# One pipeline over six layers: attention tiles and feed-forward groups interleaved, queries normalised on GpSimd, row maxima subtracted by a product on TensorE

## The reference, cut to what matters

```python
x = x + linear_attention(layernorm(x))            # once, 4 x 1024 tokens of 128
y = layernorm(x)
for i in range(6):
    y = attn_layer(shift_tokens(y), ...) + y
    y = ffn_layer(shift_tokens(y), ...) + y
return x + y

def attn_layer(x, Wqkv, qs, ksc, Wo):             # 16 heads of 64
    q, k, v = split(x @ Wqkv)
    q = l2norm(q) * qs;  k = l2norm(k) * ksc
    q = q*cos*scale + rotate_half(q)*sin*scale    # k with 1/scale
    sim = einsum(q, k) * 8                        # windows of 32, with the window before
    attn = softmax(where(mask, -max, sim))
    return einsum(attn, v).reshape(...) @ Wo

def ffn_layer(x, g, bln, W1, b1, W2, b2):         # inner width 341
    xn = layernorm(x) * g + bln
    a, gate = split(xn @ W1 + b1)
    return a * gelu(gate) @ W2 + b2
```

## Time and profile before

| | |
|---|---|
| median of 3 runs | 3576.26 us (3575.43 to 3576.86) |
| the profiled execution | 3575.57 us, span from first to last instruction 3573.7 us |
| PE busy | 3252.6 us, 91% |
| ACT busy | 2933.6 us, 82% |
| DVE busy | 2791.6 us, 78% |
| POOL busy | 2045.7 us, 57% |
| granted TensorE clock, mean | 0.958 of full speed |

### The profile page before, as it was taken

How to read it: one execution, slowest core, us unless ns; L and a number is a source line. 1 busy time by engine, 2 the same in 40 slices (tenths; PEclk the granted TensorE clock), 3 DMA queues, 4 the chain that set the end, 5 groups by cost and what they waited for, 6 DMA issues and landing times. The chain is left out here.

```text
span 3573.7 us, 118257 instructions
## 1 busy us (share of the span) xinstructions
PE 3252.6 (91%) x42076; PEld 2208.0 (62%) x42076; DVE 2791.6 (78%) x5370; ACT 2933.6 (82%) x9257; POOL 2045.7 (57%) x2150
## 2 busy tenths in 40 slices
PE   5699998889999789999789999978999977999977
PEld 4466665656666556666566666665666655666656
DVE  7788887578888568888658888757888856888865
ACT  3399998479999459999649999937999955999973
POOL 3566665456666356666446666545666634666644
PEclk8799999899999899999899999989999989999999
DMA  2000001100000100000110000010000010000011
GB/s 70 10 7 8 7 7 33 22 13 7 7 7 6 47 15 8 7 7 7 37 24 7 8 7 7 10 44 14 7 8 7 6 43 19 8 7 7 7 34 42
DMA packets 141061, 57.58 MB, mean 16 GB/s; under 512 B 118598, under 2 KB 137668, under 8 KB 139460
## 3 DMA queue, kind: packets, MB, share of 16 engines
q1 hardware_dynamic: 140484, 50.01, 5.9%
HBM read 22.57 MB, written 2.10 MB: 7 GB/s over the span
## 5 line engine op out<-in xcount | busy, mean ns | idle before, releaser
L1321 ACT ACTIVATE probs<-s_ps,nbias,rnorm 128x64 f32<-128x64 f32 x3072 | 1229.9, 447 | 1.6 <-DVE nbias L1039 0.9
L1524 POOL TENSOR_TENSOR qk_rot<-by_cos,by_sin 128x1024 f32<-128x1024 f32 x384 | 914.0, 2380 | 381.9 <-DVE by_sin L989 334.8
L597 PE MATMUL ring<-wvo,xsT 128*32 128x512 f32 x6144 | 794.8, 600 | 10.2 <-ACT vo L1144 10.2
L1321 ACT ACTIVATION_READ_ACCUMULATOR probs<-s_ps,nbias,rnorm 128x1 f32 x3072 | 765.0, 249 | 0.0
L1513 POOL TENSOR_TENSOR probs<-probs,rrow 128x256 f32<-128x256 f32 x768 | 454.6, 613 | 429.1 <-DVE rrow L973 429.1
L986 DVE TENSOR_TENSOR by_cos<-qk_ps,rotary 128x1024 f32<-128x1024 f32 x378 | 463.0, 1225 | 147.1 <-ACT squares L1307 147.1
L1533 POOL TENSOR_TENSOR qk_rot<-qk_rot,rnorm 128x1024 f32<-128x1024 f32 x192 | 365.5, 1904 | 341.4 <-DVE rnorm L733 341.4
L543 PEld LDWEIGHTS ring<-cst,qk_rot 128*128 128x128 f32 x3072 | 341.3, 141 | 243.7 <-ACT vo L1144 155.9
L543 PE MATMUL ring<-cst,qk_rot 128*128 128x128 f32 x3072 | 446.4, 278 | 27.6 <-POOL qk_rot L1524 24.4
L1001 DVE TENSOR_REDUCE sumsq<-squares 128x16 f32<-128x1024 f32 x384 | 462.9, 1206 | 0.0
L989 DVE TENSOR_TENSOR by_sin<-qk_ps,rotary 128x1024 f32<-128x1024 f32 x378 | 459.2, 1215 | 0.0
(11 more groups left out here) (166 smaller groups left out, 5433.4 us busy)
## 6 DMA issues: line engine op xcount, KB each, us to landing
qk_rot<-L_ffn_Wqkv SPq DMA_DIRECT2D x7, 1024.0 KB, 5.1
xs<-x_tok SPq DMA_DIRECT2D x194, 32.0 KB
xs<-x_tok SPq DMA_DIRECT2D x194, 31.8 KB
by_cos<-x_tok SPq DMA_DIRECT2D x48, 128.0 KB
by_cos<-x_tok SPq DMA_DIRECT2D x48, 127.0 KB
wv<-L_ffn_Wqkv SPq DMA_DIRECT2D x7, 512.0 KB, 6.6
wo_pad<-L_ffn_Wo SPq DMA_DIRECT2D x14, 256.0 KB, 7.3
xs<-x_tok SPq DMA_DIRECT2D x194, 0.2 KB
```

The lines of the kernel that those rows point to most:

```text
L597: last = mm(r[WIN * mh:WIN * (mh + 1), :], xsT[:, a, WIN * w:WIN * (w + 1)], wvo[:, mh, :, :], start=True, stop=True)
L1321: last = nc.scalar.activation(probs[:, a, h // 4, :, h % 4, :], s_ps[:, half, c:c + 2 * WIN].rearrange("p (s c) -> p s c", s=2), ACT.Exp, ...
L1524: g.tensor_tensor(qk_rot[:, n, :], by_cos[:, n, :], by_sin[:, n, :], ALU.add).then_inc(added[qk], 1)
```

## The change

The loop over layers is gone; every engine's list is written out for all of the program, 202 steps. A step still has the parts of the attention tiles, and now also parts of feed-forward groups: group U starts in step 6 + 4U, three steps after its last tile entered (the step in which that tile's residual is added), and moves through eight steps, while attention goes on with later tiles of the same layer and of the next. A step of kind f (0 to 3) is a step `6 + 4U + f`; kind 0 and 4 of one group fall together, and so on.

```diff
+        def group(k, f):
+            u, rest = divmod(k - LAST_RESIDUAL - f, FT)      # 6 + f, 4
+            return u if rest == 0 and 0 <= u < GROUPS else None
...
+                down(group(k, 6))
+                up("gate", 2, group(k, 3))
+                project("k", 0, 1)
+                project("k", 1, 1)
+                for part, at_step in NEXT_VALUES:            # steps 14, 15, 18, 19, 22, 23 of a layer
+                    next_values(next_layer_at(k, at_step), part)
+                values(2, 2)
+                transposed("q", 1, 2)
+                transposed("q", 0, 2)
+                values(1, 2)
+                transposed("k", 0, 2)
+                up("up", 0, group(k, 3))
+                up("up", 1, group(k, 3))
+                values(0, 2)
+                transposed("k", 1, 2)
+                probs_transposed(0, 3)
+                xs_transposed(0)
+                scores(0, 2)
+                normalised_transposed(group(k, 2))
+                project("q", 0, 0)
+                project("q", 1, 0)
+                up("up", 2, group(k, 4))
+                probs_transposed(1, 3)
+                values(3, 2)
+                scores(1, 2)
+                shift(0, 2)
+                output(3)
+                up("gate", 0, group(k, 2))
+                up("gate", 1, group(k, 2))
+                shift(1, 2)
```

The softmax is put together otherwise. DVE writes the negated row maxima, PE adds them to the scores in PSUM, ACT takes the exponentials with no scale, bias or sum, four heads at a time, and DVE sums the rows. The query norms can then no longer be the exponential's scale, so POOL multiplies the queries by them:

```diff
+                def shift(half, s):
+                    pe.wait_ge(max_done[half], done(T))
+                    mm(s_ps[:, half, :], ident_r[:, :], nmax[:, 8 * half:8 * half + 8].unsqueeze(2)
+                       .broadcast_to([P, 8, 2 * WIN]), start=False, stop=True, ...).then_inc(shifted[half], 1)
...
-                        for h in (h0, h0 + 1):
+                    act.wait_ge(shifted[half], done(T))
+                    for q in range(2):
+                        last = nc.scalar.activation(
+                            probs[:, a, 2 * half + q].rearrange("p s h c -> p h s c"),
+                            s_ps[:, half, 256 * q:256 * q + 256].rearrange("p (h s c) -> p h s c", h=4, s=2), ACT.Exp)
...
+                def row_sums(half, s):
+                    dve.wait_ge(exp_done[half], done(T))
+                    v.tensor_reduce(psum_row[...], p, AXY, ALU.add).then_inc(row_summed[half], 1)
...
-                    add_rotated("q", 0)
-                    add_rotated("k", 0)
-                    normalise_k(0)
-                    normalise(0, 1)
-                    normalise(1, 1)
+                normalise(1, 2)
+                add_rotated("q", 0)
+                next_wqk_lower(next_layer_at(k, NT - 1), 0)
+                squared4(group(k, 0))
+                normalise_rotated("q", 0)
+                add_rotated("k", 0)
+                x_and_bias(group(k, 2))
+                normalise_rotated("k", 0)
+                group_rsqrt(group(k, 0))
+                normalise(0, 1)
+                next_wqk_lower(next_layer_at(k, NT - 1), 1)
```

1516 lines of the change are left out of this document (756 added, 760 removed).

## The result

| | before | after |
|---|---|---|
| median | 3576.45 us (4 runs) | 3762.48 us (4 runs, 3761.50 to 3763.90) |
| ratio | | 1.0521, 95% interval 1.0503 to 1.0539 |
| span of the profiled execution | 3573.7 us | 3761.5 us |
| PE, ACT, DVE, POOL busy | 91, 82, 78, 57% | 93, 61, 81, 65% |
| mean granted clock | 0.958 | 0.984 |

The changed kernel is 5.2% slower. The forecast of 3512 us is missed by 250 us, and the range (3370 to 3690) by 72.

The account below looks back on a forecast made before the run. PE and ACT both full in attention; the prize was 122.8 us a layer outside it. Front 148, 48 groups of 67.9 (3259), values 22, seam 30, ramps 51: 3510 us of span, 3512 us forecast; eight in ten 3370 to 3690.

Parts of the forecast that it names:

- The failed step on DVE: On DVE, the second small operation comes 0.08 us before POOL's pair ends and was expected to go in between.
- the rival with 0.27: DVE's small operations wait for the port POOL holds: a miss costs PE 1.5 us, 3600 to 3795 us; chance 0.27.
- The failed step on PE: On PE, a tile keeps its pieces at 14.00 us and gets two shifts, becoming 14.6 us.
- the two shifts: On PE, two added products of 512 columns a tile, 0.31 us each, 0.62 together.
- the waits besides the port: PE held 1.3 us for the group's token scaling and 0.6 for gelu's table load, per four tiles.
- what is paid once a layer: At each layer's seam: next layer's values 4.5 us, five times 22; POOL's weight splitting 30 us in all.
- The late scaling in the step of kind 2: POOL's sum delays DVE's scaling of the group's tokens, holding PE's transposes 1.3 us; bounds 0 and 3.4.
- Gelu's table: On ACT, the load ahead of gelu delays the keys' squares; 0.6 us charged a group, bounds 0 and 1.28.
- A group's own products: On PE, a feed-forward group's transposes, W1 and W2 products: together 7.5, say 7.6 us.
- A period above 69.2 us: Sign on PE: four tiles and a group taking longer than this make the kernel slower than before; 67 to 69 expected.
- the 95% given: Sign: PE busy above 95% through the whole middle, with ACT and POOL at 70 to 75%.
- the sign named for the rival: PE waiting at L573 for DVE's rotation would show the slower port rival, chance 0.27.

Follow-up runs that it names:

- e1: Changed kernel with DVE's first two small operations of the inverse norms moved ahead of the reciprocal that POOL waits for: 3621.2 us, 1.0130 to before.
- e14: Changed kernel with PE's order of e6, everything else as it was, DVE's small operations too: 3707.7 us, 1.0367 to before.
- e18: e12 with queries projected ahead of the group's token transposes on PE, but DVE's small operations ordered as in the changed kernel: 3640.9 us, 1.0187 to before.
- e6: e5 with values 1 moved on PE directly behind values 2, ring order and ACT's copies to match: 3550.4 us, 0.9938 to before.
- e7: e6 with gelu replaced by the square, which needs no table of its own (output differs): 3521.7 us, 0.9856 to before.
- e5: e1 with PE's first-half shift ahead of the second half's scores and the last values behind them, joining the last blocks: 3589.0 us, 1.0042 to before.
- e12: e6 with ACT's copy of the transposed tokens moved ahead of the queries' squares, and three buffers for them: 3500.0 us, 0.9790 to before.

## Why the prediction was wrong, point by point

**The failed step on DVE.** "It comes 0.08 us before POOL's pair ends, and then I expect it to go in between." The mechanism and the place were in the text as the rival with 0.27; the order of two events 0.08 us apart was guessed from pitches of other pairs of instructions. The first small operation starts 0.19 us behind the reciprocal and not 0.12, and POOL's sum 1.41 behind it and not 1.46, so L785 comes 0.02 to 0.05 us after the sum instead of 0.08 before it. In 154 of 192 steps it takes 2 us or so; in 31 of the 48 steps of kind 2 it is ahead of the sum and stays short. It costs 141 us (e1), 157 and 164 by e14 and e18: 0.73 to 0.85 us a step, half of the 1.5 that the rival had. The Trainium skill ("SBUF — State Buffer", Who interferes with whom) says that whoever issues first holds the shared pair for the whole instruction. By that rule, the trace agrees: 2.38 us when POOL's sum is first, 0.18 when POOL is idle. Where L785 starts less than 0.02 us ahead of the sum, the trace has both outcomes, 14 times each.

**The failed step on PE.** "A tile keeps its pieces and gets two shifts." The pieces were kept, not their neighbours. With 14 changes of shape instead of 6 they cost 14.73 us and not 14.0; the changes that the two shifts bring lift those from 0.62 to 0.71. Against 16.5 us a tile e1 shows 17.31: 0.81 x 192 = 155 us. It could be read before: mask to scores is 0.31 us (407.09 to 407.40 in the earlier trace rows), projection to projection 0.24:

```profile
405.29 0.40 PE L531 MATMUL qk_ps<-wqk_hi,xsT_lo 128*128 128x512 f32 x1
405.53 0.39 PE L529 MATMUL qk_ps<-wqk_hi,xsT_hi 128*128 128x512 f32 x1
```

I took the first for the price of a product standing alone, and so the shift, 0.31 forecast and 0.35 in e1, came out about right for another reason. With this step failed and the small operations first (e1) the kernel is 1.3% slower than before; with the port's waits alone on top of the forecast (3512 + 141 = 3653) it would have been slower as well, and e18, with PE's better order, is 1.9% slower.

**The sum.** 3510 of span; PE's pace +155, the port's waits +141; against it the waits besides the port: 1.9 us a group were charged, and in e1's last layer PE's gaps are 2.00 us in four groups, 0.5 each, -67. That makes 3739, and 22 us of the span of 3761.5 are left. Part of them is what is paid once a layer: in e1 eight groups with a seam among them take 571.8 us (transposes L683 at 346.9 and 918.6), 13.7 more than eight of the last layer's (279.05 / 4 = 69.76 each), where 9.4 was forecast (values and seam): 4.3 x 5 = 21. The rival "slower by the port" had a range of 3600 to 3795, and 3762 lies in it, but by luck: the port has half of the size given there, and the rest is PE's pace, which no rival had.

**About right.** The late scaling in the step of kind 2 was forecast at 1.3 us. PE's wait for it (L683) is 51.7 us in the changed kernel, 63.0 in e6 and 33.0 in e1, of which 10.5 to 10.7 are one wait at the program's end: 0.88, 1.11 and 0.47 us a group for the others. The mechanism, a scaling that meets POOL's sum, shows in full in e6, where L824 takes 1.51 us in the median against 0.68 undisturbed; in the changed kernel it takes 0.82, and in some groups it is only late. Gelu's table: 0.6 forecast, 0.60 in e7; the loads are 95 inside the pipeline at 1.28 us. The 2.7 us that the prediction took for a load from the Trainium skill ("ScalarE: Activation LUTs", What ACT_TABLE_LOAD costs) are there a load of 1.283 us and a drain of about 1.38. The load agrees with the trace's 1.283; a drain does not show, the next activation starts 0.01 us behind the load. A group's own products: 7.6 forecast, 7.5 by their starts in e1. The clock stays at 1.00. A period above 69.2 us makes the kernel slower: e1, with 69.8, is slower, e6, with 68.5, faster; but e5, with 276.20 / 4 = 69.05, is 0.4% slower too, so the edge lies a little lower.

**The signs.** Through the middle (348 to 3335 us) PE is busy for 2836.8 of 2987 us, 95.0%, at the edge of the 95% given; ACT (63%) and POOL (66%) there are below 70 to 75. PE's wait for DVE's rotation at L573, the sign named for the rival, is 4.5 us only: the late DVE shows as waits for L1115 (59.2) and L996 (43.9), which stand behind L785 in its list.

## What to carry to other kernels

When work is interleaved, count what stands next to what: on TensorE each change between full and quarter products, on VectorE and GpSimd each small SBUF operation that may arrive while the other holds the port. Put such operations where the other engine is waiting by construction, not where it ends by 0.1 us; and read an instruction's guards in the code before moving it. Here, two small operations moved, blocks joined, a copy moved with a third buffer for it, and a projection moved into a wait made a kernel of 3762 us one of 3477.

## What the runs showed that I had not expected

A change between full and quarter products costs 0.13 to 0.16 us by itself and some 0.12 in the pipeline, with 512 columns as with 128; full kinds among themselves and quarter kinds among themselves cost nothing. And a saving of 0.46 us a tile (88 us in all) on an engine that is busy for 99% of the time gave 32 us, a third of itself; e12, which removes a wait that had come up with it, gave 50 more.
